# Attention: probabilities kept in float32 as the stationary operand of the product with the values

## The reference, cut to what matters

```
Q, K, V = heads(x @ q_proj.T), heads(x @ k_proj.T), heads(x @ v_proj.T)   # (4, 16, 256, 16)
scores = where(causal, -inf, einsum('bhqd,bhkd->bhqk', Q, K) / sqrt(16))
out = einsum('bhqk,bhkd->bhqd', softmax(scores), V)
x = layernorm(x + out.reshape(4, 256, 256) @ o_proj.T)
```

## Time and profile before

| | before |
|---|---|
| time, median of 3 runs | 330.65 us (329.75 to 332.02) |
| profiled execution | 328.5 us, span 326.4 us |
| PE, PEld busy | 244.8 us, 166.1 us |
| DVE, ACT, POOL busy | 205.6, 147.8, 131.1 us |
| mean granted clock of PE | 0.895 of full speed |

### The profile page before, as it was taken

How to read it: one execution, slowest core, us unless ns; L and a number is a source line. 1 busy time by engine, 2 the same in 40 slices (tenths; PEclk the granted TensorE clock), 3 DMA queues, 4 the chain that set the end, 5 groups by cost and what they waited for, 6 DMA issues and landing times.

```text
span 326.4 us, 6175 instructions
## 1 busy us (share of the span) xinstructions
PE 244.8 (75%) x2095; PEld 166.1 (51%) x2096; DVE 205.6 (63%) x447; ACT 147.8 (45%) x234; POOL 131.1 (40%) x169
## 2 busy tenths in 40 slices
PE   4785787877856454356788637498999999999990
PEld 3454566656645342114577632145666656666670
DVE  4868798998998795652577759113544454454541
ACT  4451879798797863124566310033232223332220
POOL 8300265756999994540233347300221121222222
PEclk9999999999999755586999755699999999999997
DMA  6999062422334332729500002240000000000000
GB/s 213 335 297 284 12 255 67 131 69 80 113 93 128 116 99 87 206 82 259 212 1 3 0 13 81 71 118 29 18 2 18 3 10 16 16 16 16 9 6 7
DMA packets 17417, 29.31 MB, mean 90 GB/s; under 512 B 2092, under 2 KB 12910, under 8 KB 17392
## 3 DMA queue, kind: packets, MB, share of 16 engines
q1 hardware_dynamic: 15952, 25.81, 26.3%
q0 software_dynamic: 1440, 3.17, 2.7%
HBM read 19.69 MB, written 10.03 MB: 91 GB/s over the span
## 4 chain that ended last, share of the span: by engine, by line
PE 49%; DVE 19%; POOL 11%; issue 8%; ACT 7%; DMA 3%; SPq 1%; POOLq 0%; ACTq 0%; DVEq 0%
PE ps L1114 33%; DVE arena L848 3%; POOL sorted L415 3%; POOL arena L432 3%; PE ps L1421 3%; DVE wf_lo L686 2%; PE ps L1120 2%; DVE arena L826 2%; POOL sorted L455 2%; POOL arena L428 2%; PE ps L1184 1%; DMA ring<-wqkvT 1%; PE ps L1381 1%; DVE arena L845 1%; PE ps L1238 1%
## 5 line engine op out<-in xcount | busy, mean ns | idle before, releaser
L1114 PE MATMUL ps<-wf_hi,arena 128*128 x336 | 82.0, 329 | 2.8 <-DVE arena L1042 1.6
L1114 PE MATMUL ps<-wf_lo,arena 128*128 x168 | 55.2, 328 | 0.0
L1114 PEld LDWEIGHTS ps<-wf_hi,arena 128*128 128x128 f16 x336 | 32.8, 98 | 26.8 <-issue 6.9
L639 ACT ACTIVATE arena<-ps 128x512 f32<-128x512 f32 x22 | 13.1, 597 | 65.3 <-PE ps L1114 65.3
L432 POOL TENSOR_TENSOR arena<-arena 128x512 f16<-128x512 f32 x30 | 38.8, 1313 | 4.7 <-ACT arena L539 4.6
L428 POOL TENSOR_TENSOR arena<-arena 128x512 f16<-128x512 f32 x16 | 20.5, 1281 | 38.2 <-ACT arena L534 38.2
L461 POOL TENSOR_SCALAR veps<-mv 128x1 f32<-128x1 f32 x11 | 2.5, 225 | 79.3 <-DVE mv L1062 79.3
L1042 DVE SCALAR_TENSOR_TENSOR arena<-ps,arena 128x512 f32<-128x512 f32 x22 | 15.2, 692 | 25.4 <-ACT arena L639 13.5
L686 DVE SCALAR_TENSOR_TENSOR wf_lo<-ring,wf_hi 128x1024 f16<-128x1024 f32 x17 | 28.1, 1667 | 0.9 <-ACT wf_hi L484 0.8
L1120 PE MATMUL ps<-wf_hi,ones 128*128 128x512 f16 x51 | 19.0, 545 | 11.4 <-issue 5.0
L1114 PE MATMUL ps<-xT_hi,arena 128*128 x88 | 20.4, 297 | 5.4 <-DVE arena L1002 4.7
(11 more groups left out here) (205 smaller groups left out, 580.0 us busy)
## 6 DMA issues: line engine op xcount, KB each, us to landing
ring<-Wf SPq DMA_DIRECT2D x17, 512.0 KB, 3.7
sorted<-fill SPq DMA_DIRECT2D x1, 4515.0 KB, 22.8
arena<-Wf SPq DMA_DIRECT2D x7, 512.0 KB, 7.2
arena<-sorted SPq DMA_DIRECT2D x22, 129.0 KB, 2.2
sorted<-fill SPq DMA_DIRECT2D x1, 1419.0 KB, 7.0
ring<-xT SPq DMA_DIRECT2D x4, 256.0 KB, 5.0
X<-x_tok SPq DMA_DIRECT2D x1, 1024.0 KB, 7.4
ring<-ctxT SPq DMA_DIRECT2D x2, 512.0 KB, 3.8
```

The lines of the kernel that those rows point to most:

```text
L639: a.activation(sg[:, half * 512:(half + 1) * 512], ps[:, 2 * half, :], ACT.Silu, scale=1 / W_SCALE).then_inc(sg3, 1)
L1114: last = t.matmul(dst, xs(k), ws(k), start=(k == 0 and m == 0), stop=(k == nk - 1 and m == 2))
```

## The change

The probabilities are kept only in float32, in two buffers, and the values too, 16 columns and the ones: 17. The product is one float32 matmul where there were two 16-bit ones. So the float16 exponentials, POOL's subtractions, DVE's L946, the low part of the values (the third instruction of `proj_lo`) and the sum L867 go. POOL's loop over the steps goes; the scatters of the first two sequences stand in its queue with only their own waits. Three orders change as well: DVE's `outputs` takes the block of two steps back at the head of the step, ahead of `maxima`, and `o_lo` stands after the chunk split; `max_T` moves from the third to the fourth step of a sequence; and on PE `out_T` and `max_rows` stand after `scores`, just ahead of `values`.

```
-        Vs = carve([NT, H, 2 * DK + 2], F16)
-        Pf = carve([3, G * P], F32)
-        Ph = [carve([3, G * P], F16) for _ in range(2)]
-        Pl = [carve([3, G * P], F16) for _ in range(2)]
+        Vs = carve([NT, VROW], F32)
+        Pf = [carve([3, G * P], F32) for _ in range(2)]
...
 (POOL)
-            for n in range(STEPS):
...
-                g.tensor_tensor(Pl[n % 2][:, 0], Pf[:, 0], Ph[n % 2][:, 0], ALU.subtract).then_inc(p_lo, 1)
-                if n < STEPS - 1:
-                    pool.wait_ge(exped, 4 * n + 4)
-                    for c in range(1, 3):
-                        g.tensor_tensor(Pl[n % 2][:, c], Pf[:, c], Ph[n % 2][:, c], ALU.subtract).then_inc(p_lo, 1)
...
+            for b in range(B - 2):
+                pool.wait_ge(mv1, TB * (b + 1))
+                inv_std(mv[:, :, 1], TB, rs1)
+                scatter2(b)
...
 (ACT, exps)
-                a.activation(Ph[n % 2][:, 0], ps[:, 3, :], ACT.Exp, scale=DK ** -0.5).then_inc(exped, 1)
...
-                a.activation(Pf[:, 0], ps[:, 3, :], ACT.Exp, scale=DK ** -0.5).then_inc(exped, 1)
+                a.activation(Pf[n % 2][:, 0], ps[:, 3, :], ACT.Exp, scale=DK ** -0.5).then_inc(exped, 1)
                 act.wait_ge(st_rdy, 2 * n + 2)
-                a.activation(Ph[n % 2][:, 1:3], ps[:, 4:6, :], ACT.Exp, scale=DK ** -0.5).then_inc(exped, 1)
...
-                a.activation(Pf[:, 1:3], ps[:, 4:6, :], ACT.Exp, scale=DK ** -0.5).then_inc(exped, 1)
+                a.activation(Pf[n % 2][:, 1:3], ps[:, 4:6, :], ACT.Exp, scale=DK ** -0.5).then_inc(exped, 1)
...
 (DVE, outputs)
-                v.tensor_reduce(Oa, o[:, :, 0:2 * DK].rearrange("p a (s c) -> p a c s", s=2),
-                                AX.X, ALU.add).then_inc(o_read, 1)
+                link(v.reciprocal(inv_sum, o[:, :, :, DK]))
...
+                v.tensor_tensor(dst, o[:, :, :, 0:DK], inv_sum.unsqueeze(3).to_broadcast([P, TB, G, DK]),
+                                ALU.mult).then_inc(o_norm, 1)
...
 (DVE, the steps)
+                if step >= 2:
+                    outputs(step - 2)
                 if step + AHEAD < STEPS:
                     maxima(*divmod(step + AHEAD, NG))
-                if step >= 1:
-                    if b >= 1 and g == 1:
-                        o_lo(b - 1)
-                    outputs(*divmod(step - 1, NG))
-                if g == 2 and b + 1 < B:
+                if g == 3 and b + 1 < B:
                     max_T(b + 1)
...
 (PE, values)
-                pe.wait_ge(p_lo, 3 * n + (3 if n < STEPS - 1 else 1))
+                pe.wait_ge(exped, 2 * n + 2)
                 if g == 2 and b + 1 < B:
                     pe.wait_ge(mT_done, b + 2)
...
                 if n >= 1:
                     pe.wait_ge(o_norm, n)
...
-                        todo = [(p, c, kt) for c, kt in parts for p in (Ph, Pl)]
-                        for m, (p, c, kt) in enumerate(todo):
-                            last = t.matmul(dst, p[n % 2][:, c, i * P:(i + 1) * P],
-                                            Vs[:, TB * b + kt, h, 0:w],
-                                            start=m == 0, stop=m == len(todo) - 1)
+                        for m, (c, kt) in enumerate(parts):
+                            last = t.matmul(dst, Pf[n % 2][:, c, i * P:(i + 1) * P], Vs[:, TB * b + kt, at_:at_ + VW],
+                                            start=m == 0, stop=m == len(parts) - 1)
...
 (PE, the steps)
-                if g == 3 and b + 1 < B:
-                    max_rows(b + 1)
-                if b >= 1 and g == 1:
-                    out_T(b - 1)
...
                 if step + AHEAD < STEPS:
                     scores(*divmod(step + AHEAD, NG))
+                if b >= 1 and g == 1:
+                    out_T(b - 1)
+                if g == 3 and b + 1 < B:
+                    max_rows(b + 1)
                 if step >= 1:
-                    values(*divmod(step - 1, NG))
+                    values(step - 1)
```

More of the change, by code:

```diff
@@ L31 @@
 SLOT = 64
+VW = DK + 1
+VROW = H * VW
 ROW = D + 2
@@ L195, in build @@
             "s_rdy", "maxed", "mT_rdy", "mT_done", "m_row"))
-        st_rdy, exped, p_lo, av_rdy, o_read, o_norm = (sem(n) for n in (
-            "st_rdy", "exped", "p_lo", "av_rdy", "o_read", "o_norm"))
+        st_rdy, exped, av_rdy, o_norm = (sem(n) for n in (
+            "st_rdy", "exped", "av_rdy", "o_norm"))
         oT_rdy, oT_hi, oT_lo, wo_rdy, res1, bn1, mv1, rs1, x1_rdy = (sem(n) for n in (
@@ L225, in build, with v_heads @@
         bank_kT, bank_qT = bank_qk, bank_v
+        def v_heads(tt):
+            return Vs[:, tt, 0:H * VW].rearrange("p (h c) -> p h c", h=H)
         def bank_mT(b):
@@ L564, in _ @@
                     exps(b, g)
+                if b >= 1 and g == 1:
+                    o_hi(b - 1)
                 if step == 0:
@@ L819, in proj_lo @@
                 qk = ps[:, bank_qk(tt), :].rearrange("p (s h c) -> p s h c", s=2, h=H)
-                vv = ps[:, bank_v(tt), 0:D].rearrange("p (h c) -> p h c", h=H)
-                for n, (lo, src, hi) in enumerate((
+                for lo, src, hi in ((
                         (Ks[j][:, :, 1, :], qk[:, 1], Ks[j][:, :, 0, :]),
-                        (Qs[j][:, :, 2, :], qk[:, 0], Qs[j][:, :, 0, :]),
-                        (Vs[:, tt, :, DK:2 * DK], vv, Vs[:, tt, :, 0:DK]))):
-                    dve.wait_ge(qkv_hi, 3 * tt + (2, 2, 3)[n])
+                        (Qs[j][:, :, 2, :], qk[:, 0], Qs[j][:, :, 0, :]))):
+                    dve.wait_ge(qkv_hi, 3 * tt + 2)
                     v.scalar_tensor_tensor(out=lo, in0=src, scalar=1 / W_SCALE, in1=hi,
@@ L856, in max_T, with outputs @@
                 v.tensor_copy(mT[0:2 * PAIRS, :], ps16(bank_mT(b), slice(0, 2 * PAIRS))[:, 0:S]).then_inc(mT_done, 1)
-            def outputs(b, g):
-                n = NG * b + g
-                o = ps[:, 6, 0:TB * G * (2 * DK + 1)].rearrange("p (a c) -> p a c", c=2 * DK + 1)
+            def outputs(n):
+                b, g = divmod(n, NG)
+                o = ps[:, 6, 0:TB * G * VW].rearrange("p (q a c) -> p q a c", q=TB, a=G)
                 dve.wait_ge(av_rdy, n + 1)
[L863 to L866, removed]
-                v.tensor_reduce(Oa, o[:, :, 0:2 * DK].rearrange("p a (s c) -> p a c s", s=2),
-                                AX.X, ALU.add).then_inc(o_read, 1)
-                dve.wait_ge(o_read, n + 1)
+                inv_sum = Or.rearrange("p (q a) -> p q a", q=TB)
+                link(v.reciprocal(inv_sum, o[:, :, :, DK]))
                 if g == 0 and b >= 1:
@@ L959, in _ @@
                     n += 1
+                if b >= 1 and g == 1:
+                    o_lo(b - 1)
                 if projected_at(step) is not None:
                     proj_lo(projected_at(step))
-            outputs(B - 1, NG - 1)
+            outputs(STEPS - 2)
+            outputs(STEPS - 1)
             stats1(B - 2)
@@ L1144, in stack_T @@
                 j = tt % 2
-                pe.wait_ge(qkv_lo, 3 * tt + 3)
+                pe.wait_ge(qkv_lo, 2 * tt + 2)
+                pe.wait_ge(qkv_hi, 3 * tt + 3)
                 for a in range(PAIRS):
@@ L1166, in scores @@
                     elif projected_at(step - 1) is not None:
-                        pe.wait_ge(qkv_lo, 3 * projected_at(step - 1) + 2)
+                        pe.wait_ge(qkv_lo, 2 * projected_at(step - 1) + 2)
                 if g == 0:
@@ L1318, in _ @@
                     qkv(projected_at(step))
-            values(B - 1, NG - 1)
+            values(STEPS - 1)
             out_T(B - 1)
```

51 lines of the change are left out of this document (12 added, 39 removed).

## The result

The median of the changed kernel is 373.56 us (373.38 to 376.15) against 331.33 us, +42.2 us. The ratio of the runs is 1.132, 95% interval 1.126 to 1.138 (the two medians by themselves give 1.127). The forecast was 348 us in a range of 335 to 356. The sign was right; the size was more than twice the one forecast.

A forecast was written before the change was run, and what follows sets the result against it. DVE was taken as nearest to a bound until 99.20 us, then POOL, with TensorE idle 23.1 us. Loop +18.3, ahead -1.0, behind +0.9 made +18.2, 346.7 us for the profiled execution; forecast 348 us, range 335 to 356.

The forecast's parts named there:

- The float32 product, 12 x 2 x 0.112 = 2.69 us: Values block on TensorE: 12 products of two records each, +2.09 us a block, x16 = +33.4 us.
- Rival 2: Values block: float32 records overlap in a long row like 16-bit ones, block stays 0.60 us, kernel 325.5 us; chance 0.07.
- the 0.13 us a record of the range: Values block: dearer float32 record used for the forecast case's own range, 341 to 356 us; by the walk +25.
- the 0.15 of the upper bound: Values block: the 17 columns come on top of each load, 0.15 a record, 3.6 us a block.
- The waits of the new order: Attention loop: PE waits for DVE's queue before max_rows, values and out_T; for example 9.68 us from block 2 to 3.
- the walk: Attention loop: queues followed in order at full clock; 15 values-block intervals sum to 97.3 us against 79.0, +18.3.
- Rival 1: TensorE's 23.1 us idle absorb most of the products: +5, 336 us, range 335 to 341; chance 0.13.
- The third rival: Steps 12 to 16 of the loop fall into half clock: +10, 358 us; chance 0.07.
- the signs at the end of the prediction: Expected in the profile: 2.7 us blocks, last block near 141 us, POOL about 72, ACT about 122, TensorE at full clock.
- POOL, ACT, DVE relieved: Attention loop: POOL loses 59 us of subtractions, ACT two of four exponentials a step, DVE L867, L946 and third L826s.
- Ahead of the loop, -1.0: Before the first block: DVE's third L826 goes for three token tiles on the path, -1.0 us.
- Behind the loop, +0.9: Last block costs 2.69 instead of 0.86 us; out_T, outputs and projection return about 1 us if the clock stays up.

The follow-up runs named there:

- e11: Kernel before plus 60 back-to-back float32 products of 128 columns behind its last matmul; 333.63 us in one execution.
- e13: Changed kernel with 64 instead of 17 columns in every float32 product, same queues and waits; 356.56 us, ratio to the kernel before 1.078.
- e4: Changed kernel's float32 block, with the DVE and PE order of the kernel before; 354.88 us, ratio to the kernel before 1.071.
- e7: Order of the kernel before with a float16 block of 12 products, 17 columns, low parts left out; 309.25 us, ratio to the kernel before 0.937.
- e14: Float32 products with 64 instead of 17 columns, in the order of the kernel before; 337.25 us, ratio to the kernel before 1.015.
- e9: Kernel before plus 100 back-to-back float32 products of 17 columns behind its last matmul; 360.76 us in one execution.
- e10: Kernel before plus 900 back-to-back float16 products of 17 columns behind its last matmul; 347.87 us in one execution.

## Why the prediction was wrong, by its steps

- **The float32 product, 12 x 2 x 0.112 = 2.69 us:** right at full clock. L1381 with four records in a row priced 24 in a row, also that the 17 columns lie under the load; e11 shows it up to 128. Rival 2 (cheaper records) is out. No row shows the 0.13 us a record of the range or the 0.15 of the upper bound; the runs have 0.112 at full and 0.213 at half clock.
- **The waits of the new order:** right in place and size (9.56 us against 9.68 from block 2 to 3; twelve of fifteen intervals of e13 within 0.11 us). By the walk the order costs 97.3 - 85.5 = 11.8 us at full clock. e4, e7 and e14 against their counterparts give 15 to 19 us, and in each pair the new order also has the lower clock (0.75 and 0.83, 0.84 and 0.97, 0.92 and 1.00), which the walk leaves out. Rival 1 (idle time absorbs the product) would have been about right only with the old order and a full clock: e14 is +5.7 us.
- **The clock:** the step that failed. The sum priced the loop at full clock, and the signs at the end of the prediction say so: "TensorE's clock stays at full speed through the loop". The third rival priced a loss of +10 us, in the last steps only, at a chance of 0.07 and argued against it that TensorE would be busy for most of the time. It was busy for 90%, and the clock was 0.75. The 22.0 us that the loop took beyond the walk lie here: the last block starts at 166.49 us, where 44.7 + 97.3 = 142.0 were forecast ("near 141" among the signs). e9 shows that 17-column float32 products lose the clock with no wait at all, e11 that 128-column ones keep it, and e13 that widening alone gives 17.0 us back. What remains in e13 (0.92) is half-clock stretches with wide products: each stands behind an idle wait of the new order, and e14, without these waits, has none. No run changed one wait at a time.
- **POOL, ACT, DVE relieved:** right where it mattered. POOL is 72.1 us busy (72 forecast), the last steps are no longer bound by it, and no chunk split on DVE takes more than 1.23 us, where one took 5.13. ACT is 127.7 us busy and not 122: the forecast added up the durations of exponentials whose records overlap in part.
- **Ahead of the loop, -1.0:** seen once, at full clock: the first block comes at 44.79 us in e14 (44.7 in the walk), but at 47.23 in the changed kernel, which ran from 30 to 47 us at 0.80. The change is not what did it. e9, e10 and e11 are the kernel before up to their last products, and their first blocks start at 48.6, 49.3 and 48.2 us with a clock of 0.78 to 0.89 from 30 to 45.7 us, where the execution that the prediction read starts it at 45.70 with full clock. So this stretch differs between executions of the same instructions, by up to 3.6 us; why it does stays open.
- **Behind the loop, +0.9:** from the last block's start to the end of the span it is 205.1 us against 201.6, so +3.5. The last block takes 5.1 us at half clock where 2.69 was priced, and this stretch runs at half clock in both kernels, so the 1 us that a clock at full speed was to return did not come. Once that stretch is over, at 187.0 us here and at 141.9 before, nothing differs: the rest takes 184.6 us against 184.5.

## What to carry to other kernels

Price a block of matmuls at both clocks, and ask whether its own products hold the clock: a busy share of 100% did not assure it here. A float32 product with a 128x128 stationary operand costs two loads of 0.112 us at full clock whatever streams behind them up to 128 columns, so fill the columns or avoid the type. A change of order that comes along with a change of arithmetic needs a price of its own; here it was 15 to 19 us, 11.8 of them by the walk at full clock.

## What the runs showed of the hardware

- One hundred percent busy and half clock: back-to-back products of 17 columns, float32 (e9) and float16 (e10), lost the full clock 5.7 and 5.2 us into the run and did not regain it in the 30 and 17 us looked at. Products of 128 columns (e11) kept it for their 13.3 us.
- At half clock a float32 record takes 0.213 us instead of 0.112 (e9), a float16 record of 17 columns 0.027 instead of 0.025 (e10).
- 17, 64 and 128 columns behind a 128x128 float32 load all follow at 0.112 us a record at full clock (the changed kernel, e13, e11).
- Idle waits and narrow products each cost clock by themselves: 0.83 without the new order's waits (e4), 0.92 with 64 columns in place of 17 (e13), 1.00 without both (e14), 0.75 with both.
